# A grouped convolution with a LoRA feed-forward on one core: when chunks of the weight are combined, and the order of three steps in the opening

## The chip, the cores and the metric

The kernel runs on one core of a Trainium2 chip. The metric is the device time of one execution in microseconds. The core has a matrix engine (TensorE, PE), a vector engine (VectorE, DVE), a scalar engine (ScalarE, ACT), GpSimd (POOL) and SyncE (SP). Each has its own instruction stream, and they wait for each other on semaphores only. In this kernel SyncE issues most DMAs, GpSimd issues those of the weight's combining.

## The reference

32 samples of 128 channels x 2048 positions go through a grouped convolution (4 groups, 9 taps) with a context added, then through a dense layer of 2048 x 2048 with bias and two LoRA terms: one with A and B mixed per batch of 4 samples by a gate over 16 experts, one shared. The input is added at the end.

```python
def cond(x, c, weight, c_weight, bias):
    out = conv_general_dilated(x, weight, stride 1, pad 4, feature_group_count=4)
    return out + einsum('nd,od->no', c, c_weight)[:, :, None] + bias[None, :, None]

def ffn(x, gate, kernel, bias, lora_A, lora_B, lora_A_shared, lora_B_shared):
    base = x @ kernel + bias
    A_eff = einsum('bn,nri->bri', gate, lora_A)
    B_eff = einsum('bn,nor->bor', gate, lora_B)
    delta = einsum('bor,btr->bto', B_eff, einsum('bri,bti->btr', A_eff, x))
    delta += einsum('or,btr->bto', lora_B_shared, einsum('ri,bti->btr', lora_A_shared, x))
    return base + delta

out = x + ffn(cond(x, ...), ...)
```

## The kernel before, in words

Everything is float32. A product of two float32 operands is made of three matmuls on parts: each operand is split into a high and a low part (a copy to a rounded type on ScalarE, a subtraction on VectorE).

The dense layer is computed with seven block products in place of eight. The weight is cut into quarters B11, B12, B21, B22, and the seven products need sums and differences of the quarters, called T4 to T7 (L116). They are **formed** in the opening of the program, in eight chunks j = 0 to 7. For each chunk, GpSimd loads four tiles of 512 KB, one of each quarter, into `g[:, 2]` to `g[:, 5]` (L677) and stores four combinations to HBM (L680). It loads chunk j + 1 only when all stores of chunk j have landed, since there is one set of buffers. VectorE makes the combinations in place, with four subtractions or additions (L1020, L1021 in a first half, L1024, L1026 in a second). `FORM_AT` (L46) says in which step which halves are made; `form(j, half)` (L1016) waits for the chunk's load.

The program is a sequence of seven phases of 16 steps (`NP`), u = 0 to 111. A step is 48 matmuls of one sample pair with a block of the weight (`product`, L1439), with other work threaded into it. In phase 0 (u = 0 to 15) TensorE does in each step: the convolution of the next sample (`conv`, L1315, 72 matmuls in four groups), the product, within it the LoRA A part (`ax_part`, L1362), the turning of one sixteenth of lora_B (`turn_lora_B`, L1372), and at the step's end the mixing of it with the gate (`mix_B`, L1379). `conv(v)` waits before its fourth group for the copy of the last mixed lora_B (`bmix_copied`, L1309); `ax_part(u)` waits for the first evacuated group of the next convolution (L1358).

VectorE in a step of phase 0, in this order: split of lora_A (L1042, every other step), rearranging of x for a later sample (`x_rearrange`, L955, eight copies), evacuation of the convolution with the context added (`y_evacuate`, L971, four), the low parts of x (L961) and of y (L1032), the sum of the LoRA A part (`sum_ax`, L1078, L1089), the copy of mixed lora_B out of PSUM (`copy_mixed_B`, L1144), then the forming, then in some steps the low part of a weight tile (L947). ScalarE has the high parts, the other half of x, and the copies before and after the turning of lora_B (`perm_lora_B` L784, `copy_turn` L789).

The opening, before step 1, mixes lora_A with the gate. Its four parts of 1 MB (`load_lora_A(0)` to `(3)`, L375) hold experts' ranks; `mix_A(n)` (L1394) takes parts 0 and 1 for n = 0 to 3 and parts 2 and 3 for n = 4 to 7. ScalarE copies each result out (L800), `turn_A(n)` (L1404) transposes it, VectorE copies it out again (`copy_turned_A`, L1139), SyncE stores it (L505). Between n = 3 and n = 4 lies the convolution of sample 1. The evacuated convolution y of a sample is stored by `store_y` (L515, two tiles of 512 KB). The end of the opening is `mix_B(0)`.

Of the kernel before, what the change touches and what calls it, by code (L numbers as in the profile page):

```python
# [42 lines left out]
AX_PHASES = (0, 1, 3, 4)  # L43
EARLY_SPLIT = {5: 0, 8: 1, 11: 2}
STAGE_AT = {2: (0,), 3: (1,), 4: (2, 3), 6: (4,), 9: (5,), 12: (6,)}
FORM_AT = {2: ((0, 0), (0, 1)), 3: ((1, 0), (1, 1)), 4: ((2, 0), (2, 1)), 5: ((3, 0),), 6: ((3, 1), (4, 0))} | {  # L46
    u: ((u // 2 + 1, u % 2),) for u in range(9, 14)} | {7: ((4, 1),), 8: ((5, 0),)}


TAPS_OF = [(2, 1, 1, 0, 12, 0), (5, 0, 2, 0, 4, 12), (3, 2, 1, 0, 12, 4), (1, 0, 1, 4, 12, 0), (4, 3, 1, 0, 8, 8),  # L50
# [4 lines left out]
def build(nc, x, cond, conv_bias, conv_w, c_weight, gate, W, ffn_bias, lora_A, lora_B, lora_As, lora_Bs, out):  # L55
# [18 lines left out]
    with ExitStack() as ctx:  # L74
# [10 lines left out]
        g = sb("g", [P, 8, HALF])  # L85
# [6 lines left out]
        b_raw = sb("b_raw", [P, HALF])  # L92
# [58 lines left out]

        la_raw = [buf.rearrange("p a n -> p (a n)") for buf in (g[:, 2:4, :], g[:, 4:6, :], st[:, 0:2, :], st[:, 2:4, :])]
        gate_pair = [buf[:].rearrange("p (b k r) -> p b k r", b=NB, k=2) for buf in (ax_prev, ax_diff)]
        mixed = [buf[:, i * 512:(i + 1) * 512] for buf in (b_raw, g[:, 2], g[:, 3]) for i in range(2)]
        mixed = mixed[0:2] + mixed
        a_stage = [g[:, 6 + b].rearrange("p (q n) -> p q n", q=2 * NB) for b in range(2)]


# [13 lines left out]
        la_in = [sem(f"la_in{k}") for k in range(RK)]  # L172
# [179 lines left out]
        def _(sp):  # L352
# [17 lines left out]
            def load_lora_A(k):  # L370
                if k == 1:
                    sp.wait_ge(as_done, 1)
                elif k >= 2:
                    sp.wait_ge(w_lo_ready, 2 + 2 * k)
                sp.dma_start(la_raw[k], lora_A[:, k * R8:(k + 1) * R8, :]).then_inc(la_in[k], 16)  # L375
# [136 lines left out]
            def store_y(v):  # L512
                sp.wait_ge(y_evac, 4 * (v + 1))
                for i, dst in enumerate((A11_d, A12_d) if v < NP else (A21_d, A22_d)):
                    sp.dma_start(dst[v % NP], g[:, i]).then_inc(yc_out[i], 16)  # L515
# [12 lines left out]
            load_t(0, 7)  # L528
            load_lora_A(0)
            load_lora_A(1)  # L530
            store_y(0)
            load_lora_A(2)
            load_x(2)
# [13 lines left out]
            for u in range(1, NU):  # L547
# [24 lines left out]
                if f in (1, 3, 4):  # L572
                    n = {1: 0, 3: NP, 4: 2 * NP}[f] + p
# [109 lines left out]
        def _(act):  # L683
# [33 lines left out]
            def y_hi(u):  # L717
                f, b = u // NP, u % 2
                if u >= 2:
                    act.wait_ge(main_done, u - 1)  # L720
                    if in_ax(u - 2):
                        act.wait_ge(ax_done, ax_index(u - 2) + 1)
                if f == 0:
                    act.wait_ge(y_evac, 4 * (u + 1))
                    src = g[:, 0]
                elif f == 2:
                    act.wait_ge(s2_ready, u % NP + 1)
                    src = s2_buf
                elif f in (3, 6):
                    act.wait_ge(diff_ready, diff_index(u) + 1)  # L730
                    src = y_in_buf[b]
                else:
                    act.wait_ge(y_in[b], 16 * (y_index(u) // 2 + 1))
                    src = y_in_buf[b]
                A.copy(y_buf[b][:, :, 0, :], src.rearrange("p (k o) -> p k o", o=P)).then_inc(y_hi_ready, 1)  # L735
# [42 lines left out]
            def perm_lora_B(q):  # L778
                act.wait_ge(lb_raw_in, 16 * (q + 1))
                if q == 0:  # L780
                    act.wait_ge(ctx_out, 16)
                else:
                    act.wait_ge(bmix_out, 16 * q)
                A.copy(lora_B_perm.rearrange("p k (n r) -> p k n r", r=R8),  # L784
                       lora_B_raw.rearrange("p (n k r) -> p k n r", k=RK, r=R8)).then_inc(lb_perm, 1)
# [5 lines left out]
            def copy_mixed_A(n):  # L791

                act.wait_ge(amix_done, n + 1)
                if n == 0:
                    act.wait_ge(ctxt_done, 1)
                elif n == 1:
                    act.wait_ge(ctx_out, 16)
                elif n < 4:
                    act.wait_ge(aturn_done, n - 1)
                A.copy(mixed[n].rearrange("p (t w) -> p t w", t=4),  # L800
                       acc[:, 1, n % 2, :].rearrange("p (w t) -> p t w", t=4)).then_inc(amix_copied, 1)
# [64 lines left out]
            copy_mixed_A(5)  # L866
            x_split_half(1)
            copy_mixed_A(6)
            y_hi(1)
            copy_mixed_A(7)  # L870
            perm_lora_B(0)
            copy_turn(0)

            for u in range(1, NU):
# [42 lines left out]
                if f in (1, 4):  # L917
                    n = final_index(u)
# [22 lines left out]
        def _(dve):  # L941
# [74 lines left out]
            def form(j, half):  # L1016

                if half == 0:
                    dve.wait_ge(form_in, 64 * (j + 1))
                    V.tensor_tensor(g[:, 5], g[:, 5], g[:, 3], ALU.subtract).then_inc(form_done, 1)  # L1020
                    V.tensor_tensor(g[:, 3], g[:, 3], g[:, 2], ALU.subtract).then_inc(form_done, 1)  # L1021
                else:
                    dve.wait_ge(form_done, 4 * j + 2)
                    V.tensor_tensor(g[:, 2], g[:, 5], g[:, 2], ALU.add).then_inc(form_done, 1)  # L1024
                    dve.wait_ge(form_done, 4 * j + 3)
                    V.tensor_tensor(g[:, 4], g[:, 4], g[:, 2], ALU.subtract).then_inc(form_done, 1)  # L1026
# [84 lines left out]
            for v in range(2):  # L1111
                n = conv_sample(v)
# [106 lines left out]
            for u in range(1, NU):  # L1219
                f, p = u // NP, u % NP  # L1220
                pu, pf = u - 1, (u - 1) // NP

                if u + 1 < NU and (u + 1) // NP in (3, 6):
                    difference(u + 1)
                if pf in (2, 3):
                    evac(pu)
                if pf in (1, 4):
                    n = final_index(pu)
                    dve.wait_ge(ax_hi_ready, n + 1)
                    V.tensor_tensor(ax_hl[R2:P, pu % 2, 0, :], ax[R2:P, :], ax_hl[R2:P, pu % 2, 0, :].bitcast(F32),  # L1230
                                    ALU.subtract).then_inc(ax_lo_ready, 1)
                if pf == 4:
                    dve.wait_ge(axd_hi_ready, pu % NP + 1)
                    V.tensor_tensor(axd_hl[R2:P, 0, :], ax_diff[R2:P, :], axd_hl[R2:P, 0, :].bitcast(F32), ALU.subtract
                                    ).then_inc(axd_lo_ready, 1)
                if in_lora(pu):
                    if pu % 2 == 0:
                        b_split(pu)
                    pre_add(pu)
                if f in AX_PHASES and p % 2 == 0:  # L1240
                    a_split(u)
                if u + 1 < NU and not has_conv(u + 1):
                    y_lo(u + 1)
                if f + 1 < 7 and p == NP - 1 and not has_conv(u + 1):
                    split_t(f + 1, 3)
                    split_t(f + 1, 4)
                if next_x(u) is not None:
                    x_rearrange(next_x(u))
                if has_conv(u + 1):
                    y_evacuate(conv_index(u + 1))  # L1250
                if u == 1:
                    a_split(0)
                if has_conv(u + 1) and (u + 1) // NP == 2:
                    sums(u + 1)
                if has_conv(u + 2):
                    x_split(conv_index(u + 2))
                if has_conv(u + 1):
                    y_lo(u + 1)
                if pf == 5:
                    i = pu - 5 * NP  # L1260
                    dve.wait_ge(lora_done, lora_index(pu) + 1)
                    dve.wait_ge(u2_in[pu % 2], 16 * (i // 2 + 1))
                    V.tensor_tensor(u2_buf[pu % 2], acc_flat[pu % 2], u2_buf[pu % 2], ALU.add).then_inc(evac_u, 1)
                if in_lora(pu):
                    evac(pu)
                if u == 1:
                    sum_ax(0)
                if f in AX_PHASES:
                    sum_ax(u)
                if u < NP:  # L1270
                    copy_mixed_B(u)
                for j, half in FORM_AT.get(u, ()):
                    form(j, half)
                if u in (NP - 1, 5 * NP):
                    bias_lo(0 if u == NP - 1 else 1)
                if f + 1 < 7 and p in EARLY_SPLIT:
                    split_t(f + 1, EARLY_SPLIT[p])
                if f + 1 < 7 and p == NP - 1:
                    for c in range(3 if has_conv(u + 1) else 5, NCH):
                        split_t(f + 1, c)  # L1280
# [4 lines left out]
        def _(pe):  # L1285
# [199 lines left out]
            turn_A(3)  # L1485
            conv(1)
            mix_A(4)
            for n in range(5, 8):
                mix_A(n)
                turn_A(n - 1)  # L1490
            turn_A(7)
            turn_lora_B(0)
            mix_B(0)

            for u in range(1, NU):
# [28 lines left out]
```

## Time and profile before

| | |
|---|---|
| time, median of 3 runs | 1747.46 us (1746.62 to 1748.48) |
| the profiled execution's own time | 1745.75 us |
| its span, first to last instruction | 1743.9 us |
| granted TensorE clock, mean | 0.995 |
| busy: TensorE, its weight loads, VectorE, ScalarE, GpSimd | 99%, 84%, 57%, 38%, 2% |
| DMA | 419.48 MB, mean 241 GB/s |
| product matmuls L1439, share of the chain that ended last | 67% |
| convolution matmuls L1315, share of it | 16% |

Times are in microseconds from the span's start, those marked ns excepted. A busy engine is one with an instruction in flight. "Idle before" is the engine's own idle time in front of an instruction, and the arrow names what it waited for.

### The profile page before, as it was taken

The numbers are of one execution on the slowest core, as the hardware profiler recorded it, in microseconds if no ns is written. First come the engines' busy times: TensorE is split into PE (matmuls) and PEld (weight loads), VectorE is DVE, ScalarE is ACT, GpSimd is POOL, SyncE is SP. The second block draws the span as 40 slices with busy tenths as digits, with TensorE's granted clock in tenths as the row PEclk, the third lists the DMA queues.
The fourth block names the chain that finished last, engine by engine and source line by source line (L and its number), as shares of the span: only waits on it lengthen the run. The fifth ranks groups of instructions, "written<-read, shape, count | busy, mean of one in ns | idle before, by whom it ended". The sixth has DMA issues, their size and how long they took to land.

```text
span 1743.9 us, 21989 instructions
## 1 busy us (share of the span) xinstructions
PE 1721.3 (99%) x8666; PEld 1460.0 (84%) x8666; DVE 986.6 (57%) x1260; ACT 671.4 (38%) x846; POOL 36.2 (2%) x70
## 2 busy tenths in 40 slices
PE   8999979999999999999999999999999999999998
PEld 6788868888888899999999888888888888888887
DVE  7756756664444578777675544455455554464443
ACT  6766556663222466555561221132233211121110
POOL 0001110000000000000000000000000000000000
PEclk9999989999999999999999999999999999999999
DMA  7869767665675667766665666568677898887764
GB/s 229 254 193 330 273 214 248 216 224 172 230 239 196 209 232 264 272 253 239 249 240 207 211 242 223 191 199 268 215 227 226 274 334 307 302 321 258 242 240 159
DMA packets 180143, 419.48 MB, mean 241 GB/s; under 512 B 50692, under 2 KB 90212, under 8 KB 175400
## 3 DMA queue, kind: packets, MB, share of 16 engines
q1 hardware_dynamic: 169960, 381.22, 64.4%
q0 software_dynamic: 9216, 33.56, 5.2%
q10 hardware_dynamic: 864, 3.29, 0.5%
q8 instruction: 69, 1.13, 0.3%
q14 instruction: 34, 0.28, 0.0%
HBM read 271.97 MB, written 146.03 MB: 240 GB/s over the span
## 4 chain that ended last, share of the span: by engine, by line
PE 92%; DMA 4%; DVE 3%; issue 1%; SPq 0%; POOL 0%; ACT 0%; DVEq 0%; ACTq 0%
PE acc L1439 67%; PE cps L1315 16%; PE acc L1346 3%; PE cps L1362 3%; DMA g<-in_L_ffn_kernel 2%; DMA T<-g 1%; PE acc L1394 1%; PE cps L1379 1%; DMA g<-in_L_ffn_lora_A 1%; DVE x_q L955 0%; PE cps L1372 0%; DMA b_raw<-shared_B 0%; DMA mixed_B<-b_raw 0%; DVE g L1024 0%; POOL g L677 0%
## 5 line engine op out<-in xcount | busy, mean ns | idle before, releaser
L1439 PE MATMUL acc<-w_hi,y_t 128*128 128x512 f32 x3584 | 995.1, 391 | 0.0
L1439 PEld LDWEIGHTS acc<-w_hi,y_t 128*128 128x128 f32 x3584 | 666.3, 188 | 136.1 <-issue 2.7
L1439 PE MATMUL acc<-w_lo,y_t 128*128 128x512 f32 x1792 | 553.7, 390 | 0.0
L1439 PEld LDWEIGHTS acc<-w_lo,y_t 128*128 128x128 f32 x1792 | 337.0, 188 | 71.5
L696 ACT COPY x_q<-x_raw 32x512 f32<-32x512 f32 x248 | 268.9, 1084 | 17.3 <-DVE x_lo L961 13.1
L1072 DVE TENSOR_TENSOR g<-acc,g 128x1024 f32<-128x1024 f32 x96 | 117.2, 1222 | 201.7 <-PE acc L1346 114.6
L1315 PE MATMUL cps<-cw_hi,x_hi 128*128 128x384 f32 (+2 forms) x768 | 228.9, 298 | 0.7 <-DVE x_lo L1131 0.7
L1315 PE MATMUL cps<-cw_lo,x_hi 128*128 128x384 f32 (+2 forms) x768 | 228.9, 298 | 0.0
L1315 PE MATMUL cps<-cw_hi,x_lo 128*128 128x384 f32 (+2 forms) x768 | 228.4, 297 | 0.0
L735 ACT CAST y_t<-g 128x1024 fp32r<-128x1024 f32 x95 | 100.3, 1055 | 328.0 <-PE acc L1439 299.1
L1032 DVE TENSOR_TENSOR y_t<-g,y_t 128x1024 fp32r<-128x1024 f32 x95 | 116.0, 1221 | 103.6 <-ACT y_t L735 103.4
L1315 PEld LDWEIGHTS cps<-cw_hi,x_hi 128*128 128x128 f32 x768 | 145.2, 189 | 13.6 <-issue 11.4
L955 DVE COPY x_q<-x_raw 32x512 f32<-32x512 f32 x248 | 147.5, 595 | 3.9
L1315 PEld LDWEIGHTS cps<-cw_lo,x_hi 128*128 128x128 f32 x768 | 145.2, 189 | 0.6
L1315 PEld LDWEIGHTS cps<-cw_hi,x_lo 128*128 128x128 f32 x768 | 145.2, 189 | 0.0
L809 ACT COPY ax_tmp<-cps 64x256 f32<-64x256 f32 x64 | 23.7, 370 | 289.5 <-PE cps L1362 289.3
L1078 DVE TENSOR_TENSOR ax_tmp<-cps,ax_tmp 128x256 f32<-128x256 f32 x64 | 27.2, 424 | 156.1 <-ACT ax_tmp L810 156.0
L708 ACT CAST x_hi<-x_q 128x1040 fp32r<-128x1040 f32 x62 | 63.0, 1061 | 121.9 <-PE cps L1315 90.7
L971 DVE TENSOR_TENSOR g<-cps,ctx_bias 128x512 f32<-128x512 f32 x128 | 82.3, 686 | 41.2 <-PE cps L1315 40.0
L1362 PEld LDWEIGHTS cps<-y_t,a_parts 128*128 128x128 f32 x512 | 71.0, 191 | 17.1 <-issue 10.8
L1362 PE MATMUL cps<-y_t,a_parts 128*128 128x256 f32 x512 | 73.1, 286 | 10.8 <-DVE g L971 10.0
L947 DVE TENSOR_TENSOR w_lo<-st,w_hi 128x1024 fp32r<-128x1024 f32 x56 | 67.2, 1222 | 25.9 <-ACT w_hi L693 25.2
(121 smaller groups left out, 945.3 us busy)
## 6 DMA issues: line engine op xcount, KB each, us to landing
g<-A SPq DMA_DIRECT2D x80, 512.0 KB, 4.9
g<-U SPq DMA_DIRECT2D x80, 512.0 KB, 6.4
A<-g SPq DMA_DIRECT2D x64, 512.0 KB, 4.7
g<-in_x SPq DMA_DIRECT2D x64, 512.0 KB, 6.4
out<-g SPq DMA_DIRECT2D x64, 512.0 KB, 3.5
x_raw<-in_x SPq DMA_DIRECT2D x31, 1024.0 KB, 5.3
U<-g SPq DMA_DIRECT2D x48, 512.0 KB, 3.7
g<-in_L_ffn_kernel POOLq DMA_DIRECT2D x32, 512.0 KB, 8.6
```

What stands on the lines that cost most here:

```text
L696: return A.copy(x_q[r * GC:(r + 1) * GC, gr, :, 1:1 + P], x_raw[gr * GC:(gr + 1) * GC, r:L:S4].rearrange("p (w j) -> p j w", j=S4))
L708: A.copy(x_hi[:, 2 * i:2 * i + 2], x_q[:, 2 * i:2 * i + 2]).then_inc(x_hi_ready, 1)
L735: A.copy(y_buf[b][:, :, 0, :], src.rearrange("p (k o) -> p k o", o=P)).then_inc(y_hi_ready, 1)
L947: V.tensor_tensor(w_lo[:, k % SLOTS], st[:, k % 4], w_hi[:, k % SLOTS].bitcast(F32), ALU.subtract).then_inc(w_lo_ready, 1)
L955: ins = V.tensor_copy(x_q[r * GC:(r + 1) * GC, gr, :, 1:1 + P], x_raw[gr * GC:(gr + 1) * GC, r:L:S4].rearrange("p (w j) -> p j w", j=S4))
L971: V.tensor_tensor(y_conv[:, :, gr * GC:(gr + 1) * GC], cps[:, gr, :].rearrange("p (t o) -> p t o", o=GC), ctx_bias[:, v % 2, gr * GC:(gr + ...
L1032: V.tensor_tensor(y_buf[b][:, :, 1, :], src.rearrange("p (k o) -> p k o", o=P), y_buf[b][:, :, 0, :].bitcast(F32), ALU.subtract).then_inc( ...
L1072: V.tensor_tensor(stage[b], acc_flat[b], stage[b], ALU.add).then_inc(evac_dve, 1)
L1315: ins = T.matmul(cps[:, gr, t0 * GC:(t0 + k1 - k0) * GC], xs[:, gr, row, col:col + P], cw_strip[ws][:, gr, k0 * GC:k1 * GC], start=(n == 0 ...
L1346: ins = T.matmul(acc[:, b, m, :], ax_hl[:, b, part, :], moving[:, m * 512:(m + 1) * 512], start=False, stop=(part == 1))
L1362: ins = T.matmul(ax_ps, a_parts[:, c, :], y_buf[b][:, c].rearrange("p h r -> p (h r)"), start=(c == 0), stop=(c == NCH - 1))
L1439: ins = T.matmul(acc[:, b, m, :], y_buf[b][:, c, part, :], wt[:, k % SLOTS, m * 512:(m + 1) * 512], start=(c == 0 and part == 0 and wt is ...
```

## The change

Four places are edited.

1. `FORM_AT`: before, halves were made in steps 2, 3, 4 (two each, a whole chunk), 5 (one), 6 (second half of chunk 3 and first half of chunk 4) and 7 to 13 (one each). After: steps 2, 3, 4 (whole chunks 0, 1, 2), 5 to 10 (one half each, chunks 3 to 5), 12 and 13 (whole chunks 6 and 7). And the forming of a step stands ahead of `copy_mixed_B(u)` in VectorE's stream.
2. SyncE waits for lora_A's second part (`la_in[1]`) before it issues the store of the first y.
3. `turn_lora_B(0)` stands behind `mix_A(7)` on TensorE, ahead of `turn_A(6)` and `turn_A(7)`; `perm_lora_B(0)` stands ahead of `y_hi(1)` on ScalarE.
4. The list `mixed` is written in another way and holds the same buffers.

```diff
-FORM_AT = {2: ((0, 0), (0, 1)), 3: ((1, 0), (1, 1)), 4: ((2, 0), (2, 1)), 5: ((3, 0),), 6: ((3, 1), (4, 0))} | {
-    u: ((u // 2 + 1, u % 2),) for u in range(9, 14)} | {7: ((4, 1),), 8: ((5, 0),)}
+FORM_AT = {u: ((j, 0), (j, 1)) for u, j in ((2, 0), (3, 1), (4, 2), (12, 6), (13, 7))} | {
+    u: (((u + 1) // 2, (u + 1) % 2),) for u in range(5, 11)}
...
             load_lora_A(1)
+            sp.wait_ge(la_in[1], 16)
             store_y(0)
...
             copy_mixed_A(6)
+            perm_lora_B(0)
             y_hi(1)
             copy_mixed_A(7)
-            perm_lora_B(0)
             copy_turn(0)
...
                     sum_ax(u)
+                for j, half in FORM_AT.get(u, ()):
+                    form(j, half)
                 if u < NP:
                     copy_mixed_B(u)
-                for j, half in FORM_AT.get(u, ()):
-                    form(j, half)
...
-            for n in range(5, 8):
+            for n in range(5, 7):
                 mix_A(n)
                 turn_A(n - 1)
+            mix_A(7)
+            turn_lora_B(0)
+            turn_A(6)
             turn_A(7)
-            turn_lora_B(0)
             mix_B(0)
```

VectorE at the end of step 6 and the beginning of step 7, before:

```order
L1078 TENSOR_TENSOR ax_tmp<-cps,ax_tmp 128x256
L1089 TENSOR_TENSOR ax<-ax_tmp 128x128
L1144 COPY b_raw<-cps 64x512
L1024 TENSOR_TENSOR g<-g 128x1024
L1026 TENSOR_TENSOR g<-g 128x1024
L1020 TENSOR_TENSOR g<-g 128x1024
L1021 TENSOR_TENSOR g<-g 128x1024
L955 COPY x_q<-x_raw 32x4x128 x8
L971 TENSOR_TENSOR g<-cps,ctx_bias 128x16x32 x4
```

The same place after (`b_raw<-cps` is the copy of mixed lora_B, the rows `g<-g` are the forming):

```order
L1078 TENSOR_TENSOR ax_tmp<-cps,ax_tmp 128x256
L1089 TENSOR_TENSOR ax<-ax_tmp 128x128
L1024 TENSOR_TENSOR g<-g 128x1024
L1026 TENSOR_TENSOR g<-g 128x1024
L1144 COPY b_raw<-cps 64x512
L955 COPY x_q<-x_raw 32x4x128 x8
L971 TENSOR_TENSOR g<-cps,ctx_bias 128x16x32 x4
```

The pair L1020, L1021 of chunk 4, which stood between the second half of chunk 3 and the rearranging of x, is gone from here (it now stands at the end of step 7), and the pair that stays has moved ahead of the copy.

TensorE at the end of the opening, before (`cps<-ident,g` are the turns of lora_A, two of them in the row marked x8; `cps<-ident,b_raw` is the turn of lora_B):

```order
L1394 MATMUL acc<-st,ax_prev 128x512
L1394 MATMUL acc<-st,ax_diff 128x512
L1404 MATMUL cps<-ident,g 128x128 x8
L1372 MATMUL cps<-ident,b_raw 128x128 x4
L1379 MATMUL cps<-b_raw,G 64x512
```

And after:

```order
L1394 MATMUL acc<-st,ax_prev 128x512
L1394 MATMUL acc<-st,ax_diff 128x512
L1372 MATMUL cps<-ident,b_raw 128x128 x4
L1404 MATMUL cps<-ident,g 128x128 x8
L1379 MATMUL cps<-b_raw,G 64x512
```

The four transposes of lora_B have moved ahead of the eight of lora_A; the mix L1379 closes the stretch as before.

## Rows read from the trace of the kernel before

**Rows 1.** The page: TensorE's busy time, and the stores of y among the DMA issues.
```profile
PE 1721.3 (99%) x8666; PEld 1460.0 (84%) x8666; DVE 986.6 (57%) x1260; ACT 671.4 (38%) x846; POOL 36.2 (2%) x70
...
A<-g SPq DMA_DIRECT2D x64, 512.0 KB, 4.7
```
**Rows 2.** TensorE's waits, 0 to 420 us: waiter, releaser, total us, times, longest.
```profile
PE cps L1362 <- DVE g L971: 10.0, 2, 9.6
```
**Rows 3.** Timeline of VectorE, steps 3 to 7: start, us, instructions, idle before.
```profile
145.21 0.68 DVE L1144 COPY b_raw<-cps 64x512 f32<-64x512 f32 x1 [5.43 <-PE cps L1379]
148.30 1.22 DVE L1020 TENSOR_TENSOR g<-g 128x1024 f32<-128x1024 f32 x1 [2.41 <-DMA g<-in_L_ffn_kernel]
...
173.70 1.23 DVE L1020 TENSOR_TENSOR g<-g 128x1024 f32<-128x1024 f32 x1 [4.46 <-DMA g<-in_L_ffn_kernel]
...
178.60 4.83 DVE L955 COPY x_q<-x_raw 32x512 f32<-32x512 f32 x8
...
193.52 0.68 DVE L1144 COPY b_raw<-cps 64x512 f32<-64x512 f32 x1 [3.48 <-PE cps L1379]
197.24 1.23 DVE L1020 TENSOR_TENSOR g<-g 128x1024 f32<-128x1024 f32 x1 [3.04 <-DMA g<-in_L_ffn_kernel]
...
216.86 0.68 DVE L1144 COPY b_raw<-cps 64x512 f32<-64x512 f32 x1 [4.27 <-PE cps L1379]
...
218.71 1.23 DVE L1026 TENSOR_TENSOR g<-g 128x1024 f32<-128x1024 f32 x1
233.89 1.22 DVE L1020 TENSOR_TENSOR g<-g 128x1024 f32<-128x1024 f32 x1 [13.96 <-DMA g<-in_L_ffn_kernel]
...
252.51 0.68 DVE L1144 COPY b_raw<-cps 64x512 f32<-64x512 f32 x1 [4.89 <-PE cps L1379]
```
**Rows 4.** Timeline of TensorE in step 7.
```profile
241.87 2.04 PE L1362 MATMUL cps<-y_t,a_parts 128*128 128x256 f32 x8 [9.64 <-DVE g L971]
```
**Rows 5.** Stretch 242 to 247 us: engines' busy time, granted clock, DMA share, GB/s.
```profile
core 0: us, PE busy (x) PEld busy (x) DVE busy (x) ACT busy (x) POOL busy (x), PEclk, DMA share, GB/s
242.00:247.00 5.00, 5.00 (x19) 4.31 (x19) 5.00 (x7) 3.40 (x6) 0.00 (x0) 0.50 0.95 325
```
**Rows 6.** Chain that ended last: start, us, what; a turn of lora_B, a convolution, product matmuls.
```profile
91.96 0.44 PE cps L1372 x4
...
193.48 9.89 PE cps L1315 x72
...
203.37 5.53 PE acc L1439 x24
```
**Rows 7.** Timeline of GpSimd: the loads of chunks 2 and 3 are issued.
```profile
161.45 2.10 POOL L677 DMA_DIRECT2D g<-in_L_ffn_kernel  x4 [7.19 <-DMA T<-g]
...
182.93 2.19 POOL L677 DMA_DIRECT2D g<-in_L_ffn_kernel  x4 [3.00 <-DMA T<-g]
```
**Rows 8.** Timeline of TensorE in the opening: mixes of lora_A, mix of lora_B.
```profile
39.03 1.02 PE L1394 MATMUL acc<-g,ax_prev 128*128 128x512 f32 x2
42.48 2.07 PE L1394 MATMUL acc<-g,ax_diff 128*128 128x512 f32 x2 [2.43 <-DMA g<-in_L_ffn_lora_A]
...
73.15 1.04 PE L1379 MATMUL cps<-b_raw,G 128*64 128x512 f32 x2 [1.19 <-DVE g L1139]
```
**Rows 9.** Timeline of VectorE: the split of y of sample 1.
```profile
71.19 1.21 DVE L1032 TENSOR_TENSOR y_t<-g,y_t 128x1024 fp32r<-128x1024 f32 x1
```
**Rows 10.** Timeline of SyncE's queue: stores of y, third part of lora_A.
```profile
30.51 1.19 SPq L515 DMA_DIRECT2D A<-g  x2
32.00 0.74 SPq L375 DMA_DIRECT2D st<-in_L_ffn_lora_A  x1
```
**Rows 11.** DMA issues at 30.4 to 31 and at 31.7 to 33 us: size, issue to landing.
```profile
g<-in_L_ffn_lora_A SPq DMA_DIRECT2D x1, 1024.0 KB, 12.6
A<-g SPq DMA_DIRECT2D x1, 512.0 KB, 13.6
...
st<-in_L_ffn_lora_A SPq DMA_DIRECT2D x1, 1024.0 KB, 17.4
```
**Rows 12.** Timeline of ScalarE: the copy of the fifth mixed part of lora_A.
```profile
64.12 0.59 ACT L800 COPY g<-acc 128x512 f32<-128x512 f32 x1 [3.18 <-PE acc L1394]
```

More of the change, by code:

```diff
@@ L153, in build @@
         gate_pair = [buf[:].rearrange("p (b k r) -> p b k r", b=NB, k=2) for buf in (ax_prev, ax_diff)]
-        mixed = [buf[:, i * 512:(i + 1) * 512] for buf in (b_raw, g[:, 2], g[:, 3]) for i in range(2)]
-        mixed = mixed[0:2] + mixed
+        mixed = [buf[:, i * 512:(i + 1) * 512] for buf in (b_raw, b_raw, g[:, 2], g[:, 3]) for i in range(2)]
         a_stage = [g[:, 6 + b].rearrange("p (q n) -> p q n", q=2 * NB) for b in range(2)]
```

## The prediction

> **What bounds the kernel now.** I read the page first: TensorE is busy 99% of a span of 1743.9 us [rows 1], so only two things can shorten the program, less work for TensorE (the change has the same instructions on it) or less waiting. The view of TensorE's waits over the first quarter says where it waits: 10.0 us for the evacuation of the convolution (L971) [rows 2], and in the opening 2.4 us for a part of lora_A and 1.2 us for a copy of turned lora_A (L1139) [rows 8], and little else. All three lie where the change works. Later phases are untouched and I leave them at their time.
>
> The largest wait is best seen on VectorE [rows 3]. The copy of mixed lora_B (L1144) ends TensorE's step u, so its starts are a clock of the steps: 145.21 (step 3), 193.52 (5), 216.86 (6), 252.51 (7). Step 6 is the regular step, 216.86 - 193.52 = 23.34 us. Steps 4 and 5 take 48.31 together, 1.63 more than two regular ones; step 7 takes 35.65, 12.31 too much. The reason stands in the same rows: at the end of step 6 VectorE forms the second half of chunk 3 (last subtraction at 218.71), then wants the first half of chunk 4 and sits idle 13.96 us until that chunk has been stored, reloaded and landed. Behind it in program order stand the rearranging of x and the evacuation L971, and TensorE waits for the latter 9.64 us in front of L1362 [rows 4]. In the stretch from 242 to 247 us [rows 5] the granted clock is 0.50, the 1.2 GHz level, and the eight matmuls of L1362 take 2.04 us; so 12.31 is 9.64 of idling and 2.67 of running at the lower level after it. Steps 4 and 5 have a small form of the same thing: at the end of step 4 the subtractions start at 173.70 after waiting 4.46 us, x is rearranged only at 178.60, and the evacuation comes just too late.
>
> **Part 1, the forming steps.** Two edits work together. The table now gives step 6 only the second half of chunk 3 and step 7 the first half of chunk 4, and so on, one half a step up to step 10, nothing in step 11, whole chunks in steps 12 and 13. And forming stands ahead of L1144, not behind it.
> The table: chunk 4 is needed one step later, so it has 23.34 us more to land, against the 13.96 us that it was late. The wait in step 6 goes. The DMA loop from the end of a forming to the next chunk (233.89 - 219.94 = 13.95 us) fits into every later single-half step, and again in steps 12 and 13, where the next bound applies.
> The order: in step 3 VectorE sat idle 5.43 us before L1144, waiting for TensorE's mix [rows 3]. Four subtractions take 178.60 - 173.70 = 4.90 us, so they fit into this gap, and what follows starts about 5 us sooner. But if the chunk is late, the copy is now late with it. How late may it be? Call the mix's end M. A forming is due at M - 5.43. The loop from one whole forming to the next is limited by its DMAs and took 173.70 - 148.30 = 25.40 us, longer than a step. With the first forming at 139.78 - 23.34 = 116.44, the next start at 141.84, 167.24 and 192.64, against M = 145.21 in step 3, 168.55 in step 4 and 191.89 in step 5, each 23.34 after the last: at -3.4, -1.3 and +0.8. TensorE's next convolution takes 9.89 us [rows 6] in four groups; the fourth, 7.4 us in, waits for L1144. A whole forming (4.90) and the copy (0.68) must start by M + 1.8, a half (2.3) by about M + 4.4. The rearranging (4.9) and the first evacuation (0.7) have to be done before L1362, 9.89 + 5.53 = 15.4 us after M [rows 6], which is a later bound. So nothing waits, with 3.1 us to spare in step 4. Step 5 becomes regular as well, since in step 4 the rearranging starts at about 172.8, not 178.60.
> SyncE's queue has a wait for L1144 too. It stands 0 to 4 us longer there, before the store of mixed lora_B, the store of E and the next load of x; x was waiting for the rearranging anyway, which is now sooner.
> Gain: 12.31 + 1.63 = 13.94 us. Bounds: no gain beyond it, since no step gets shorter than 23.34. For the other end I take the slowest pieces of the loop: four subtractions 4.90; the stores of chunk 1, from the end of its forming at 153.20 until the next load begins at 161.45, 8.25; the load begun at 182.93 [rows 7] and used at 197.24 [rows 3], 14.31. Such a loop is 27.5 us, an estimate. The starts become 171.4 in step 4, 1.1 us too late, and 198.9 in step 5; by then the waits add to 116.44 + 3 x 27.5 - (191.89 + 4.4) = 2.7 us. So the part gives 11.2 to 13.9 us; I take 13.9, since the 25.40 us loop is the one measured.
>
> **Part 2, lora_B turned sooner.** TensorE turns the first part of lora_B ahead of the last two turns of lora_A, ScalarE prepares it ahead of the split of y. The end of this stretch is the mix L1379, which waited 1.19 us until 73.15 for VectorE's copy L1139 of the eighth turn [rows 8]. That copy could not begin before the split of y was done (71.19, 1.21 us) [rows 9], and the split stands directly behind the copy of the seventh turn. The seventh turn now starts one block of four transposes later, 0.44 us [rows 6]. So the copy of the seventh turn, the split and the copy of the eighth all move by 0.44 us and L1379 starts at 73.6: the move feeds an operand that wasn't late and delays the one that was. Cost: 0.44 us. The bounds: 0 if the copy of the seventh turn has slack that I don't see, 0.9 if a second block of this length gets in front of the split as well, as ScalarE's preparing of lora_B before its own half of the split could. I take +0.4.
>
> **Part 3, y stored behind lora_A's second part.** TensorE waits 2.43 us until 42.48 for this 1 MB [rows 8]; behind it in SyncE's queue stood the two stores of y and the third part of lora_A. If they took bandwidth from it, holding them back makes it land sooner. Issues and landings say otherwise. The stores of y are issued at 30.51, the third part at 32.00 [rows 10]; from issue to landing the second part takes 12.6 us, the first store of y behind it 13.6, the third part 17.4 [rows 11]. So they land at 42.4 or 42.5, when TensorE goes on, 44.1 and 49.4: in order of issue, and 7 us for the 2 MB of y and the third part. That is a queue served in turn, in which what stands behind costs nothing.
> The Trainium skill, DMA: Bandwidth & Descriptors, section on queues, rings and completion order, says that "on each SDMA engine descriptors are consumed in ring order"; by that rule this edit would bring 0 us, and by plain sharing of the bandwidth up to the 4.0 us of the rival below. The landings of the trace agree with the rule.
> I take -0.3 us, for engines that finish early and then serve y. The bounds: 2.43 us of wait plus about 1.6 us of lower clock (the pair after the wait took 2.07 us, the one before it 1.02 [rows 8]; for the next pairs I add 0.5) is the most, -4.0. The other end: the queue runs empty at 42.4. A store of y takes 4.7 us from issue as a median [rows 1], so the first would land at 47.2, not 44.1, and all behind it 3.1 us later. x of the third sample is one of those. If ScalarE waits for it now, its rearranging ends 3.1 us later; the copy L800 behind it starts at 64.12 after 3.18 us of idling [rows 12]. That is just covered; if the transfers come 1.5 us later still, TensorE waits some 1 us. So -4.0 to +1.0.
>
> **Sum.** Against the profiled execution: span 1743.9 - 13.9 + 0.4 - 0.3 = 1730.1 us, and its own time of 1745.75 becomes 1731.95. The median of the runs shown is 1.71 us above it; the prediction is the median's: 1747.46 - 13.8 = 1733.7 us. What a measurement of this kernel can tell from no change is about 0.2%, 3.5 us.
>
> **Rivals.**
> A. Holding y back does free the second part of lora_A. For: a transfer is done only with its slowest engine, and engines that are done early do serve y meanwhile, beside it. Against: the landings in order of issue. All of the 4.0 us, in place of 0.3: 1730.0 us. By the other side of this reasoning, x then also comes sooner by the same amount and does not stand in the way.
> B. The forming loop is the new bound in steps 3 to 5: the reloading of a chunk now falls beside SyncE's x and y in another phase, the copy L1144 waits behind a late forming, and TensorE in its fourth group. With the slow loop of 27.5 us: +2.7, 1736.4 us. For: the loop is longer than a step, the lateness adds up. Against: it only has to hold for three loops.
> C. The other side, slower: the same place at a higher price. With a loop of length L the waits by step 5 sum to 3L - 79.9 us. At 31.3 us they eat the 13.9, at 32.4 the kernel is slower by 3.5. At 33 us: 19.1 - 13.8 = 5.3 slower than before, 1752.8 us. Against: that is 7.6 us over the 25.40 us measured, with the same bytes to move.
> D. The wait of 9.64 us only moves: chunk 4 is formed in time, but another transfer on SyncE's queue (x, the store of y) is what the evacuation then waits for, in about half of the amount: 1733.7 + 12.31 / 2 = 1739.9 us. For: the DMAs are full in much of this phase. Against: the regular steps 8 to 13 have the same transfers and no wait.
>
> **How the numbers follow.** Forecast 63%, A 17%, B 12%, D 4%, C 2%, and 2% for a gain of some other smaller size. The range for 8 in 10 or better spans A to B with the run's own scatter of 1 us: 1729.5 to 1737.5. Faster by more than 0.2%: 63 + 17 + 12 + 4 = 96, from which I take 1 for the unknown, 95%; within 0.2%: 3%; slower 2%.
>
> **What the new profile would show.** L1144 every 23.34 us from 145 on with no step above 23.5; no wait of VectorE at L1020 in step 6, and L1362's wait of 10.0 us gone; the granted clock full around 230 to 240 us; whole formings ending just ahead of L1144 in step 2, with a DMA wait of 2 to 4 us before L1020 in steps 3 and 4. L1379 idle about 2 us, starting 0.4 later relative to the last mix of lora_A. L1394 still waiting some 2 us for lora_A with the lower clock behind it. The forecast is wrong if a step between 145 and 400 us is longer than 24 us, or if the wait at L1394 is under 1 us.

## The result and the profile after

| | median us | runs | against before, 95% interval |
|---|---|---|---|
| before | 1747.97 | 4 (1746.62 to 1750.01) | |
| changed | 1734.88 | 4 (1732.41 to 1735.28) | 0.9921 [0.9904, 0.9938] |

The kernel became 13.1 us faster (10.8 to 16.8 by the interval); 13.8 us were forecast. The changed kernel's profiled execution has a span of 1733.0 us against 1743.9.

First its steps. The timeline of VectorE (start, us, instructions, idle before), which answers to [rows 3]:

```profile
119.12 1.22 DVE L1020 TENSOR_TENSOR g<-g 128x1024 f32<-128x1024 f32 x1
...
124.64 0.68 DVE L1144 COPY b_raw<-cps 64x512 f32<-64x512 f32 x1 [0.64 <-PE cps L1379]
...
142.46 1.22 DVE L1020 TENSOR_TENSOR g<-g 128x1024 f32<-128x1024 f32 x1
...
166.57 1.23 DVE L1020 TENSOR_TENSOR g<-g 128x1024 f32<-128x1024 f32 x1 [0.69 <-DMA g<-in_L_ffn_kernel]
...
171.37 0.67 DVE L1144 COPY b_raw<-cps 64x512 f32<-64x512 f32 x1
...
194.66 0.68 DVE L1144 COPY b_raw<-cps 64x512 f32<-64x512 f32 x1 [3.16 <-PE cps L1379]
...
218.00 0.68 DVE L1144 COPY b_raw<-cps 64x512 f32<-64x512 f32 x1 [3.04 <-PE cps L1379]
...
241.34 0.68 DVE L1144 COPY b_raw<-cps 64x512 f32<-64x512 f32 x1 [3.16 <-PE cps L1379]
```

From 124.64 to 241.34 are 116.70 us, five steps of 23.34. The 35.65 of step 7 is gone, and so is the 24.97 of step 5, which in the kernel before ran from this row to 193.52:

```profile
168.55 0.68 DVE L1144 COPY b_raw<-cps 64x512 f32<-64x512 f32 x1 [3.54 <-PE cps L1379]
```

The whole formings (119.12, 142.46) sit in the gap before L1144, which has shrunk from 5.43 to 0.64 us. Only chunk 2 came after its due time, 0.69 us late, and its forming pushed the copy of step 4 by 0.05 us, to 171.37, with nobody waiting.

TensorE's waits (waiter, releaser, total us, times, longest), answering to [rows 2]; the 10.0 us of L1362 for L971 are no longer among them:

```profile
PE acc L1394 <- DMA g<-in_L_ffn_lora_A: 2.6, 1, 2.6
PE cps L1379 <- DVE g L1139: 2.1, 1, 2.1
...
PE acc L1439 <- DVE w_lo L947: 1.3, 2, 0.8
```

What is left lies in the opening, where two of the four edits are. TensorE's timeline there, answering to [rows 8]:

```profile
43.18 1.39 PE L1394 MATMUL acc<-g,ax_diff 128*128 128x512 f32 x2 [2.55 <-DMA g<-in_L_ffn_lora_A]
...
74.34 1.66 PE L1379 MATMUL cps<-b_raw,G 128*64 128x512 f32 x2 [2.15 <-DVE g L1139]
```

And its engines by stretches of 2 us (the number before the DMA share is the granted clock):

```profile
42.00:44.00 2.00, 0.82 (x2) 0.49 (x3) 1.42 (x3) 0.00 (x0) 0.00 (x0) 0.98 0.06 23
72.00:74.00 2.00, 0.20 (x2) 0.00 (x0) 2.00 (x3) 1.98 (x3) 0.00 (x0) 1.00 1.02 343
74.00:76.00 2.00, 1.66 (x3) 0.25 (x3) 0.20 (x1) 1.99 (x2) 0.24 (x1) 0.66 0.46 138
76.00:78.00 2.00, 2.00 (x8) 2.00 (x8) 1.90 (x4) 1.98 (x3) 2.00 (x4) 0.50 1.04 243
```

Two things are to be seen. Between 42 and 44 us the DMA engines are almost empty (share 0.06): the store of y was held back until lora_A had landed, and lora_A did not land sooner for it. The share had fallen before the landing already: from 41 to 43 us, while TensorE waits for this part until 43.18, the engines are nearly idle, where in the kernel before they carry the next transfers. First the kernel before, then the changed one:

```profile
41.00:42.00 1.00, 0.00 (x0) 0.00 (x0) 0.97 (x3) 0.00 (x0) 0.00 (x0) 1.00 0.96 344
42.00:43.00 1.00, 0.52 (x1) 0.50 (x2) 0.85 (x2) 0.00 (x0) 0.00 (x0) 0.70 1.05 418
...
41.00:42.00 1.00, 0.00 (x0) 0.00 (x0) 0.97 (x3) 0.00 (x0) 0.00 (x0) 1.00 0.29 74
42.00:43.00 1.00, 0.00 (x0) 0.00 (x0) 0.97 (x3) 0.00 (x0) 0.00 (x0) 1.00 0.08 33
```

So in the kernel before other transfers do run beside the end of lora_A's, as the prediction supposed, but in engines that had little left to do for it. And behind the wait of 2.15 us at L1379 the granted clock falls to 0.50, the 1.2 GHz level; in the kernel before, after a wait of 1.19 us, it was 1.00 in the same place.

The DMA issues at 31 to 31.7 us and at 43 to 44 us (size, issue to landing), answering to [rows 11]:

```profile
g<-in_L_ffn_lora_A SPq DMA_DIRECT2D x1, 1024.0 KB, 12.6
...
A<-g SPq DMA_DIRECT2D x2, 512.0 KB, 3.3
```

12.6 us, to the tenth what it was with y behind it. That the tenth agrees is luck: in the six experiments below that leave y and lora_A where they were, the second part took 12.8 to 14.0 us. But there the first part, issued with it, took longer too. The second part took 2.7 to 3.8 us longer than the first in the seven profiles with y behind it, and 3.1 and 3.3 us in the two with y held back. A gain of a few tenths of a microsecond can't be told from this; one of the 2.4 us of the wait would show. The stores of y take 3.3 us instead of some 14: what they waited for was their turn. ScalarE, answering to [rows 12], shows what the delay cost behind it:

```profile
55.98 8.66 ACT L696 COPY x_q<-x_raw 32x512 f32<-32x512 f32 x8 [3.32 <-DMA x_raw<-in_x]
64.87 0.58 ACT L800 COPY g<-acc 128x512 f32<-128x512 f32 x1 [0.23 <-PE acc L1394]
```

x of the third sample comes at 55.98, and the idle time before the copy L800 has shrunk from 3.18 to 0.23 us. The cover was used up to a quarter of a microsecond. In the profile of part 3 alone (below) it was used up whole, and TensorE still did not wait.

### The profile page after: what moved, and what is told of

Read it like the earlier page. It is cut to its first block, busy times and chain, and to the rows that moved or that the text cites. A ratio compares the mean times of both kernels' runs of the same rounds, so it can differ in the third digit from the quotient of the medians.

```text
span 1733.0 us, 21990 instructions
## 1 busy us (share of the span) xinstructions
PE 1719.0 (99%) x8666; PEld 1458.7 (84%) x8666; DVE 989.5 (57%) x1260; ACT 668.3 (39%) x846; POOL 36.8 (2%) x70
## 4 chain that ended last, share of the span: by engine, by line
PE 97%; DMA 1%; DVE 1%; SPq 0%; ACT 0%; issue 0%; ACTq 0%
PE acc L1439 69%; PE cps L1315 18%; PE cps L1362 3%; PE acc L1346 3%; PE cps L1379 1%; PE acc L1394 1%; DMA g<-in_L_ffn_lora_A 1%; PE cps L1372 0%; DMA b_raw<-shared_B 0%; DMA mixed_B<-b_raw 0%; PE acc L1416 0%; DVE w_lo L947 0%; DVE x_q L1124 0%; PE cps L1404 0%; SPq L646 0%; DVE cw_lo L1117 0%
## 5 line engine op out<-in xcount | busy, mean ns | idle before, releaser
L1439 PEld LDWEIGHTS acc<-w_lo,y_t 128*128 128x128 f32 x1792 | 336.3, 188 | 71.3
L696 ACT COPY x_q<-x_raw 32x512 f32<-32x512 f32 x248 | 267.5, 1079 | 20.3 <-DVE x_lo L961 13.1
L971 DVE TENSOR_TENSOR g<-cps,ctx_bias 128x512 f32<-128x512 f32 x128 | 83.8, 687 | 64.6 <-PE cps L1315 63.7
L1061 DVE TENSOR_TENSOR g<-g 128x1024 f32<-128x1024 f32 x64 | 77.8, 1216 | 3.7 <-DMA g<-U 3.2
L961 DVE TENSOR_TENSOR x_lo<-x_q,x_hi 128x1040 fp32r<-128x1040 f32 x62 | 74.2, 1236 | 6.5 <-ACT x_hi L708 6.5
```

Source lines behind the costliest of these rows:

```text
L696: return A.copy(x_q[r * GC:(r + 1) * GC, gr, :, 1:1 + P], x_raw[gr * GC:(gr + 1) * GC, r:L:S4].rearrange("p (w j) -> p j w", j=S4))
L961: V.tensor_tensor(x_lo[:, 2 * i:2 * i + 2], x_q[:, 2 * i:2 * i + 2], x_hi[:, 2 * i:2 * i + 2].bitcast(F32), ALU.subtract).then_inc(x_lo_re ...
L971: V.tensor_tensor(y_conv[:, :, gr * GC:(gr + 1) * GC], cps[:, gr, :].rearrange("p (t o) -> p t o", o=GC), ctx_bias[:, v % 2, gr * GC:(gr + ...
L1061: V.tensor_tensor(stage[b], stage[b], xres[b], ALU.add).then_inc(pre_added, 1)
L1439: ins = T.matmul(acc[:, b, m, :], y_buf[b][:, c, part, :], wt[:, k % SLOTS, m * 512:(m + 1) * 512], start=(c == 0 and part == 0 and wt is ...
```

## The experiments

Twelve kernels ran. My theory: part 1 is the whole gain, part 2 costs, part 3 does nothing. The first five take the change apart; the ratio is each kernel's to the kernel before on the same chip. Each has one profile. Where two experiments are compared by their medians, they may have run on different chips, and differences of 1 to 3 us between them are near what the runs can tell.

**Part 1 alone.**

```diff
+ new FORM_AT; form(j, half) ahead of copy_mixed_B(u)
  (store_y(0), perm_lora_B(0), turn_lora_B(0) as before)
```

> The kernel before with part 1 alone (table of formings and forming ahead of the copy of mixed lora_B). My theory: this part is the whole gain, 13.9 us, in steps 4, 5 and 7; the opening keeps its times, with L1379 waiting 1.2 us and the clock full behind it. Expected 1733.5 us, and 1 to 2 us faster than the changed kernel. Rival (the opening's two edits bring part of the 13 us): 1735 us or more.

Measured: 1733.54 us against 1747.51, ratio 0.9923 [0.9912, 0.9935]: 14.0 us. It gives what the whole change gives; the two ratios (0.9923 and 0.9921) don't show the 1 to 2 us by which I expected it to be faster. Its profile shows what the prediction's rival B was about (VectorE, steps 3 to 6):

```profile
143.59 1.23 DVE L1020 TENSOR_TENSOR g<-g 128x1024 f32<-128x1024 f32 x1 [0.46 <-DMA g<-in_L_ffn_kernel]
...
171.05 1.23 DVE L1020 TENSOR_TENSOR g<-g 128x1024 f32<-128x1024 f32 x1 [4.58 <-DMA g<-in_L_ffn_kernel]
...
197.29 1.22 DVE L1020 TENSOR_TENSOR g<-g 128x1024 f32<-128x1024 f32 x1 [7.48 <-DMA g<-in_L_ffn_kernel]
199.57 0.68 DVE L1144 COPY b_raw<-cps 64x512 f32<-64x512 f32 x1
...
218.58 0.68 DVE L1144 COPY b_raw<-cps 64x512 f32<-64x512 f32 x1 [2.96 <-PE cps L1379]
```

The loop took 27.46 and 26.24 us here, and chunk 3 was 7.48 us late. The mix of step 5 was done by 218.58 - 23.34 = 195.24; the half forming started 2.05 us after it, less than the 4.4 allowed, and no step is longer.

**Part 2 alone, lora_B turned sooner.**

```diff
+ turn_lora_B(0) behind mix_A(7); perm_lora_B(0) ahead of y_hi(1)
```

> The kernel before with lora_B turned sooner alone (part 2). My theory: L1379 waits about 2.1 us instead of 1.2, because the split of y moves 0.4 us or more, and the granted clock behind it can fall to 0.5 for some us, as in the changed kernel's profile: 0.4 to 2.6 us slower, 1749 us. Rival (the edit does what it says and lora_B's copy was late): 0.4 us faster.

Measured: 1749.73 against 1747.51, ratio 1.0010 [1.0000, 1.0020]. Slower by 2.2 us in the medians, with an interval (0 to 3.5 us) that touches zero. The profiles show it more sharply, as the section on the prediction tells. The wait at L1379 is 2.1 us again, and in the stretches from 76 to 80 us the granted clock is 0.56 and 0.58.

**Part 3 alone, y held back.**

```diff
             load_lora_A(1)
+            sp.wait_ge(la_in[1], 16)
             store_y(0)
```

> The kernel before with the store of y held back alone (part 3). My theory: lora_A's second part is served ahead of y in any case, so it lands 12.6 us after its issue as before, TensorE waits 2.4 us, x of the third sample lands 3 to 4 us later and is just covered: 1747.5 us, within 1 us of before. Rival A (y took bandwidth): up to 4 us faster.

Measured: 1748.56 against 1747.51, ratio 1.0005 [0.9997, 1.0014]; the wait for lora_A is 2.6 us. Rival A is dead: by the interval at most 0.5 us is gained, and 4 us would have been seen.

**The table alone, and the order alone.**

```diff
+ new FORM_AT; form still behind copy_mixed_B           (table)
+ old FORM_AT; form ahead of copy_mixed_B               (order)
```

> The kernel before with the new table alone, forming still behind the copy of mixed lora_B. My theory: the 12.3 us of step 7 go, the 1.6 us of steps 4 and 5 stay, and chunk 7 is formed some 4 us later in step 13, which may hold SyncE and then the turn of lora_B in step 14 by up to 2 us: 1735.2 to 1737 us. Rival (the order alone matters, an earlier forming): little gain here.

Measured: 1735.71, ratio 0.9932 [0.9920, 0.9943], 11.8 us. The long step is gone and the step from 170.58 to 196.17 is still 25.59. The loss that I thought possible in step 14 did not come.

> The kernel before with the forming ahead of the copy of mixed lora_B, but with the old table. My theory: steps 4 and 5 lose their 1.6 us, but in step 6 the copy L1144 now stands behind the forming that waits for chunk 4, and TensorE waits for it in front of the convolution's fourth group: about 8.4 us and some 2.6 us at the lower clock, in place of the 12.3 us at L1362. About 3 us faster than before: 1744.5 us, with the long wait of TensorE at L1315 for L1144. Rival (the order alone brings most of the gain): 1735 us.

Measured: 1741.37 against 1747.26, ratio 0.9965 [0.9953, 0.9978]: 5.9 us, twice what I expected. TensorE's timeline shows the wait at the place named, but shorter:

```profile
229.60 0.69 PE L1315 MATMUL cps<-cw_hi,x_hi 128*128 128x384 f32 x1 [5.67 <-DVE b_raw L1144]
```

5.67 us instead of 8.4; I did not put down how the 8.4 was made up, so which term was off stays open. Why the same missing chunk costs 9.6 us of idling before and 5.7 here can be read from VectorE:

```profile
212.27 1.23 DVE L1026 TENSOR_TENSOR g<-g 128x1024 f32<-128x1024 f32 x1
226.60 1.23 DVE L1020 TENSOR_TENSOR g<-g 128x1024 f32<-128x1024 f32 x1 [13.10 <-DMA g<-in_L_ffn_kernel]
```

The second half of chunk 3 is now formed ahead of the mix and done at 213.50, so chunk 4 is there at 226.60: 10.2 us after the start of step 7's convolution (216.43), where it was 17.1 before (233.89 against 216.75). That is 7 us sooner. What has become worse is the place of the copy: TensorE needs it 7.4 us into the convolution, while the evacuation is needed only 15.4 us after the mix. Neither edit does the whole work of the other; 11.8 and 5.9 add up to more than the 14.0 of both, since both shorten step 7.

**How far the lateness may go.** A whole chunk in each of the steps 2 to 9.

```diff
+FORM_AT = {u: ((u - 2, 0), (u - 2, 1)) for u in range(2, 10)}
```

> Part 1 with a whole chunk formed in every step from 2 to 9, ahead of the copy of mixed lora_B. My theory: the forming loop takes 24.1 to 27.5 us (seen in steps 2 to 5 of the runs), the step 23.34, so the forming comes later in each step; no wait until it starts 1.8 us after the mix, 7.2 us behind its due time, from then on TensorE waits at L1315 for L1144 by the excess of each loop. With a mean loop of 26 us: 7 x 2.66 - 7.2 = 11.4 us of waits, about 1745 us; with 24.1 none. So the table's single halves in steps 5 to 10 are what keeps the lateness down. Rival (the loop's length is set by the steps' own traffic and adapts): no waits, 1733.5 us.

Measured: 1743.11 against 1748.36, ratio 0.9965 [0.9946, 0.9985], with single runs from 1732.7 to 1747.0 us. That is 9.6 us more than part 1 alone in the medians, 8.7 if each is taken against its own kernel before. In the profiled execution the formings start at 117.15, 141.82, 168.12, 194.56, 218.82, 244.11, 269.53 and 296.10 us, a mean loop of 25.6, and TensorE waits (this kernel's lines are one less):

```profile
PE cps L1314 <- DVE b_raw L1143: 5.6, 4, 1.9
```

All four waits are in front of the convolution's fourth group, behind the last four formings. The forming at 194.56 is 7.4 us behind its due time (117.15 + 3 x 23.34 = 187.17) and costs nothing; the next is 8.3 us behind and TensorE waits 0.5 us. So the lateness decides from 7.8 us on, not from 7.2.

```profile
194.56 1.23 DVE L1019 TENSOR_TENSOR g<-g 128x1024 f32<-128x1024 f32 x1 [7.31 <-DMA g<-in_L_ffn_kernel]
...
218.82 1.23 DVE L1019 TENSOR_TENSOR g<-g 128x1024 f32<-128x1024 f32 x1 [5.83 <-DMA g<-in_L_ffn_kernel]
```

With that bound 7 x 25.56 - 7 x 23.34 - 7.8 = 7.8 us were due. 5.6 us of them are these waits; the other 2.2 are steps that themselves took longer than 23.34, 1.75 us of it in the one behind the wait at 275.05, where the granted clock fell:

```profile
274.00:279.00 5.00, 3.95 (x18) 3.95 (x18) 4.91 (x8) 0.45 (x1) 0.53 (x1) 0.66 0.97 321
```

The wide scatter of the single runs would fit with loops that are short in some executions and long in others, but only this one has a profile.

**Is the queue served in turn?** Two places for the same 1 MB of y.

```diff
 (same queue, ahead of the second part)
             load_lora_A(0)
+            store_y(0)
             load_lora_A(1)
-            store_y(0)
 (on ScalarE's queue, in place of SyncE's)
+            for i, dst in enumerate((A11_d, A12_d)):
+                act.dma_start(dst[0], g[:, i]).then_inc(yc_out[i], 16)
```

> The kernel before with the store of y issued ahead of lora_A's second part on the same queue. My theory (served in order of issue): lora_A's second part lands later by what 1 MB of y takes, 3 to 4 us; TensorE waits about 6 us at L1394, and 3 to 5 us slower than before in all. Rival (they share alike): no change in the wait.

Measured: 1750.99 against 1748.36, ratio 1.0016 [1.0007, 1.0025], 2.6 us slower. The second part takes 15.2 us instead of 12.6 to 14.0, 5.1 longer than the first instead of 2.7 to 3.8, and TensorE waits for it:

```profile
46.72 2.08 PE L1394 MATMUL acc<-g,ax_diff 128*128 128x512 f32 x2 [5.78 <-DMA g<-in_L_ffn_lora_A]
```

> The kernel before with the store of y issued on ScalarE's queue, at the same time as before, so that it is not behind lora_A's second part but beside it. My theory (what stands behind in one queue costs nothing, what is in another queue shares): y lands at about 38 us or before instead of 44, lora_A's second part 2 to 4 us later than 42.5; TensorE waits 4.5 to 6 us at L1394; with the two issues on ScalarE 2 to 5 us slower than before. Rival (transfers in flight share alike, whatever their queue): the wait at L1394 stays 2.4 us.

Measured: 1750.96, ratio 1.0016 [1.0006, 1.0025]. Issues and landings of y on ScalarE's queue, and of lora_A's second part (issue at 29.0 to 29.7 and at 31.3 to 32 us):

```profile
A<-g ACTq DMA_DIRECT2D x1, 512.0 KB, 6.9
...
g<-in_L_ffn_lora_A SPq DMA_DIRECT2D x1, 1024.0 KB, 14.7
```

y's first half lands after 6.9 us instead of 13.6, its second after 11.2. lora_A's second part takes 14.7, its first 11.1 (9.4 to 10.8 in the seven kernels with y behind), and TensorE waits 4.0 us for the two, less than the 4.5 to 6 expected. That y on another queue takes from lora_A is likely from this and from the 2.6 us in the medians, but not clean: y was issued at 29.47 here, sooner than both parts of lora_A (29.75) and sooner than in the kernel before (30.51), and ScalarE had two issues more. So the positions of one store: behind in the same queue 12.6 to 14.0 us, held back 12.6 and 12.7; on another queue and somewhat sooner 14.7; ahead in the same queue 15.2.

**What would the opening need?** Two ideas: issue lora_A's first part among the weight tiles, where the DMAs were idle for half of the time (the stretch 25 to 28 us has a DMA share of 0.54 before); and take the split of y out of the way of the copy that L1379 waits for. e6, e7 and e9 have part 1 and don't hold y back; e8 has the old forming steps.

```diff
 (e6, e7: the first part ahead of the sixth tile)
+            load_lora_A(0)
             load_t(0, 5)
...
-            load_lora_A(0)
 (e9: behind the sixth tile)
             load_t(0, 5)
+            load_lora_A(0)
...
-            load_lora_A(0)
 (e7, e8, e9: lora_B sooner, and)
-            y_lo(1)
             copy_turned_A(7)
             copy_mixed_B(0)
+            y_lo(1)
```

> Part 1, and lora_A's first part issued right behind the fifth weight tile, ahead of the sixth to eighth; y not held back, lora_B turned as before. My theory (the queue is served in turn): the queue had little to do between 25 and 28 us, all of the same data then goes earlier, lora_A's second part lands at about 38.6 instead of 42.5, and TensorE's wait of 2.4 us at L1394 and the lower clock behind it go: 4 us less than part 1 alone, 1729.5 us. Rival (bandwidth bounds the landing, the bytes ahead of it are the same, so the order doesn't matter, or a weight tile comes late instead): 1733.5 us.

Measured: 1732.18, ratio 0.9911 [0.9897, 0.9924]: 1.4 us less than part 1 in the medians, which the intervals don't tell from zero, and not 4. The wait for lora_A is gone, another has come:

```profile
36.68 0.73 PE L1439 MATMUL acc<-w_hi,y_t 128*128 128x512 f32 x2 [2.66 <-DVE w_lo L947]
39.92 1.22 PE L1439 MATMUL acc<-w_hi,y_t 128*128 128x512 f32 x2 [1.35 <-DVE w_lo L947]
```

The sixth weight tile took 8.1 us from issue, 3.6 in the kernel before, and the product waited for low parts, 4.0 us in all; from 38 to 44 us the granted clock is 0.50. My theory had no price for the tiles; the megabyte ahead of them moved them by 4.5 us. Here the rival was nearer.

> The kernel before with lora_B turned sooner and the split of y moved behind the two copies, nothing else. My theory: L1379 waits under 1 us and no lower clock follows; 0.6 us faster than before, and about 2.5 us faster than with lora_B turned sooner alone. Rival: as slow as that one, 1749.7 us.

Measured: 1746.76 against 1747.26, ratio 0.9996 [0.9987, 1.0005]: unclear against before, but 3.0 us less than part 2 alone in the medians (2.7 with each against its own kernel before). The wait at L1379 is 1.0 us, and between 72 and 76 us the clock is 1.00. With the split out of its way, turning lora_B sooner costs nothing. The same profile has something that the length of the waits doesn't explain, a wait of 2.3 us for lora_A with the full clock behind it:

```profile
43.50 1.12 PE L1394 MATMUL acc<-g,ax_diff 128*128 128x512 f32 x2 [2.29 <-DMA g<-in_L_ffn_lora_A]
...
44.00:46.00 2.00, 2.00 (x6) 0.90 (x5) 0.00 (x0) 1.31 (x2) 0.00 (x0) 1.00 1.08 313
```

> As the kernel with lora_A's first part sooner, and lora_B turned sooner as in the changed kernel, but with VectorE's split of y behind the copies of the eighth turn of lora_A and of the first mixed lora_B. My theory: the split was what L1379 waited for; with it out of the way the mix starts some 0.6 us sooner than in the kernel before and the clock stays full: 1728.9 us. Rival (turning lora_B sooner is itself what costs): 1 to 2 us slower than without it.

Measured: 1731.16, ratio 0.9906 [0.9893, 0.9920], 1.0 us less than without the two moves, with single runs that overlap, and 2.3 us more than the 1728.9 expected. The waits for weights are still there, 3.5 us.

> Part 1, lora_B turned sooner with the split of y out of the way, and lora_A's first part issued behind the sixth weight tile (one tile later than in the two runs before, where the sixth tile took 8.1 us instead of about 3.6 and TensorE waited 4.0 us for weights). My theory: 1 MB ahead of the seventh tile only, which has 5 us until it is used: the waits for weights fall to about 1.5 us, lora_A's second part lands at 39 to 40 us and is not waited for: 1729.5 us. Rival (any order of the same bytes in this stretch gives one total wait): 1731 us, as the run before.

Measured: 1729.80 against 1748.36, ratio 0.9893 [0.9878, 0.9908]. Its four runs (1729.24 to 1730.22) are all below the changed kernel's (1732.41 to 1735.28): 5 us better than it in the medians, 18.6 than before. TensorE's waits in the first 450 us:

```profile
PE acc L1439 <- DVE w_lo L947: 1.9, 2, 1.4
PE acc L1416 <- DVE g L1101: 1.5, 1, 1.5
PE cps L1379 <- DVE g L1139: 1.0, 1, 1.0
```

lora_A is not waited for any more, the weight tiles cost 1.9 us, and the granted clock is 1.00 from 36 to 48 us. Both ends of the opening's loss are smaller: the idling and the slow matmuls after it.

## Why the prediction was right, point by point

- **Which wait ends last.** Right. The steps were read off L1144, the loss of 13.94 us was put into steps 4, 5 and 7, and every step is 23.3 to 23.4 now. Part 1 alone: 14.0 us measured.
- **The forming fits into the gap.** Right. The one loop that the changed kernel's profile shows waiting for its DMAs took 24.1 us, those of part 1 alone 23.9, 27.5 and 26.2; the value taken (25.40) lies among them and the slow bound (27.5) occurs. It did not cost its 2.7 us, because only the sum counts: 77.6 us for three loops, where waits were to begin at 79.9. I had forecast a DMA wait of 2 to 4 us before L1020 in steps 3 and 4; the changed kernel's profile has none and 0.69.
- **Part 2.** The delay was right, the price was not: 2.0 us, outside the bounds of 0 to 0.9. The start of L1379 moved by 0.44 us relative to the start of sample 1's convolution, as worked out: from 52.61 to 73.15 is 20.54 before, from 53.36 to 74.34 is 20.98 after. The term left out is the clock. The chain of the changed kernel's profile reads:

```profile
74.34 1.66 PE cps L1379 x2
76.01 10.85 PE cps L1315 x72
```

  where it was 1.04 and 9.89 before: 0.62 + 0.96 = 1.6 us. So part 2 costs 2.0 us in that execution, not 0.4. I had priced the lower clock for the two other waits and not for the one that the change lengthened. The time from the start of sample 1's convolution to the copy L1144 of step 2 shows it in each profile: 69.3 us in the kernel before and in the profiles of part 1, part 3, the table and e6; 71.2 and 71.3 in the two with the edit as it is; 68.6 in e7 and e8, which move the split. In the profile of part 2 alone L1379 waits 2.15 us too, and the two rows are

```profile
75.40 1.11 PE cps L1379 x2
76.51 11.35 PE cps L1315 x72
```

  So it is the longer wait and what follows it, and the split of y is what makes it long. How long a wait the clock bears is not settled: it fell behind 2.15 us here and stayed full behind 2.29 in e8.
- **Part 3.** Right: nothing gained that the runs can tell; 0.3 us they can't tell either way. The cost behind it was 3.7 us on x, 3.1 forecast, and it was just covered.
- **The sum.** -13.9 + 2.0 + 0 is -11.9; the profile shows -10.9 in the span. Of the 1.0 us between them, 0.75 lies ahead of that convolution (53.36 against 52.61), 0.58 of it before any edit acts: the first mix of lora_A starts at 39.61 instead of 39.03, with two short waits for weight tiles in this execution. Between the medians the difference is 13.1 us. What is left is within the scatter of single runs: the total came out nearer the forecast than its terms, since the 1.6 us left out of part 2 are small against an interval of 10.8 to 16.8, and that is luck.
- **Rivals.** A fell with part 3 alone. B's lateness is real and harmless with this table; e12 shows the place and the point from which it costs. C did not come near. D: no other transfer took over.

Not settled: why the loop's length varies, within one execution as well, from about 24 to 27 us (23.9 to 27.5 in part 1 alone, 24.3 to 26.6 in e12). I did not try to separate the stores from the loads in it.

## What to carry to other kernels

When one engine takes a piece of work that waits for a DMA, price what stands behind it in program order, not the wait: moving the piece by one step was worth 12 us, putting it ahead of an already idle gap 2 us more. Before holding a transfer back to help another, compare the landings with the order of issue; if they agree, hold nothing back and look for an earlier idle stretch to issue the wanted one in. And wherever an edit lengthens a wait of TensorE, add the matmuls that run at the lower clock after it: here the mix started 0.44 us later, its wait grew by 0.96 us, and the slower matmuls behind it cost another 1.6.

## What the runs showed of the hardware that I had not expected

- A transfer held back did not make the one ahead of it in the queue land sooner: lora_A's second part took 12.6 and 12.7 us with nothing behind it, 12.6 to 14.0 with y and more behind it (2.7 to 3.8 us longer than the part ahead of it, against 3.1 and 3.3). With y ahead of it in the queue it took 15.2.
- A read of 1 MB ends with a stretch in which the DMA engines do little: in the changed kernel their share is 0.29 and 0.08 between 41 and 43 us, and TensorE goes on with the data only at 43.18. In the kernel before other transfers fill that stretch (0.96 and 1.05), and the read takes the same 12.6 us.
- TensorE's granted clock does not follow from the length of the wait alone. In the opening it fell to the 1.2 GHz level behind both waits of 2.15 us and each one of 2.4 us or more, and stayed full behind waits of 1.0 to 1.2 us, and behind one of 2.29 (e8). In e12 it fell behind waits of 1.49 and 1.87 us and stayed full behind one of 1.74. What else decides is open.
